# Counting a graph's edges band by band: the last turned tiles moved amid a band, the next band's bounds taken from this band's, and a first sum whose tiles follow their parts one by one

## The reference, cut to what matters

```python
out_deg = segment_sum(ones, src); in_deg = segment_sum(ones, dst)
h_src   = h * rsqrt(clip(out_deg, 1))[:, None]
agg     = segment_sum(h_src[src], dst)            # layer 0; the others sum likewise
agg     = agg * rsqrt(clip(in_deg, 1))[:, None]
out     = elu(agg @ weight + bias)
...
m   = segment_sum(xt[src], dst) * Binv[:, None]   # layer 2 sums there and back, twice
out = segment_sum(m[dst], src) * Dinv[:, None]
```

## Time and profile before

| what | value |
|---|---|
| median of 3 runs | 1943.09 us (1941.39 to 1947.62) |
| the profiled execution's own time | 1939.86 us |
| its span | 1938.1 us |
| TensorE, matmuls | 1755.6 us, 91% of the span |
| VectorE | 949.9 us, 49% |
| ScalarE | 482.1 us, 25% |
| GpSimd | 494.8 us, 26% |
| data moved | 535.59 MB, mean 276 GB/s |

### The profile page before, as it was taken

The page is one execution under the profiler, slowest core; times in us unless marked ns, Lnnn a source line. Parts: engine busy times, 40 slices in busy tenths (PEclk is TensorE's granted clock), DMA queues, the critical chain, the costliest instruction groups (busy, mean ns, idle before and its releaser), DMA issues.

```text
span 1938.1 us, 35033 instructions
## 1 busy us (share of the span) xinstructions
PE 1755.6 (91%) x9478; PEld 1416.2 (73%) x9479; DVE 949.9 (49%) x2851; ACT 482.1 (25%) x1262; POOL 494.8 (26%) x899
## 2 busy tenths in 40 slices
PE   4888887699989999999999999999999699999971
PEld 2355555588878878888887887887777589988851
DVE  7876664444446511122211117776777544444466
ACT  0134445322223211122221111112121133232223
POOL 1122222311113300000000002226888843332314
PEclk7999999799999999999999999999999799999986
DMA  5067778899969988887768889997777399999981
GB/s 135 34 280 310 321 332 356 302 323 324 307 225 374 346 292 290 264 226 214 211 196 289 289 269 278 290 287 245 266 251 264 124 307 371 371 372 371 374 308 67
DMA packets 339452, 535.59 MB, mean 276 GB/s; under 512 B 17871, under 2 KB 275322, under 8 KB 332442
## 3 DMA queue, kind: packets, MB, share of 16 engines
q1 hardware_dynamic: 329514, 516.24, 79.4%
q0 software_dynamic: 7888, 17.23, 2.4%
q10 hardware_dynamic: 1952, 0.95, 0.3%
HBM read 405.95 MB, written 128.41 MB: 276 GB/s over the span
## 4 chain that ended last, share of the span: by engine, by line
PE 63%; SPq 13%; DVE 7%; issue 7%; DMA 5%; DVEq 2%; POOL 1%; ACT 1%; ACTq 0%; POOLq 0%
PE psum L1118 44%; PE psum L1215 6%; SPq L486 4%; PE psum L1010 4%; PE psum L1007 3%; PE psum L1029 2%; SPq L500 2%; DMA blk<-counts_src_on_rows 2%; SPq L492 2%; SPq L496 2%; SPq L489 2%; PE psum L1197 2%; PE psum L1226 1%; SPq L827 1%; DMA expert_weights<-expert_rows_out 1%
## 5 line engine op out<-in xcount | busy, mean ns | idle before, releaser
L1118 PE MATMUL psum<-xsa,blk 128*128 128x512 f32 x2500 | 638.0, 403 | 12.3 <-DVE xsa L1684 9.1
L1118 PEld LDWEIGHTS psum<-xsa,blk 128*128 128x128 f32 x2500 | 456.6, 189 | 99.8 <-issue 12.0
L1118 PE MATMUL psum<-xsb,blk 128*128 128x512 f32 (+1 forms) x1875 | 407.8, 366 | 10.4 <-DMA blk<-counts_src_on_rows 5.8
L1118 PEld LDWEIGHTS psum<-xsb,blk 128*128 128x128 f32 x1875 | 315.7, 190 | 64.4 <-issue 10.2
L1966 POOL TENSOR_SCALAR ve<-mv 128x1 f32<-128x1 f32 x75 | 16.9, 225 | 763.0 <-DVE mv L1660 763.0
L1545 DVE TENSOR_SCALAR onehots<-counts_scratch 128x348 bf16<-128x348 f16 x464 | 162.3, 376 | 85.1 <-issue 44.8
L1007 PE MATMUL psum<-onehots 128*128 128x349 bf16 x464 | 147.7, 318 | 38.6 <-DVE onehots L1550 38.0
L1010 PE MATMUL psum<-zrow 128*128 128x512 bf16 x464 | 174.1, 385 | 0.0
L592 PE MATMUL psum<-route,expert_weights 128*128 128x128 f32 x1296 | 166.2, 282 | 2.6 <-DVE route L704 2.0
L592 PEld LDWEIGHTS psum<-route,expert_weights 128*128 128x128 f32 x1296 | 154.3, 195 | 12.3 <-issue 4.6
L604 PE MATMUL psum<-expert_weights,route 128*128 128x256 f32 x648 | 153.5, 380 | 0.2
(11 more groups left out here) (317 smaller groups left out, 2113.5 us busy)
## 6 DMA issues: line engine op xcount, KB each, us to landing
blk<-counts_src_on_rows SPq DMA_DIRECT2D x125, 832.0 KB, 5.8
blk<-counts_src_on_rows SPq DMA_DIRECT2D x125, 768.0 KB, 4.7
expert_weights<-in_L_gnn_w SPq DMA_DIRECT2D x162, 512.0 KB, 8.2
blk<-counts_dst_on_rows SPq DMA_DIRECT2D x50, 832.0 KB, 6.0
counts_dst_on_rows<-band_rows SPq DMA_DIRECT2D x25, 1600.0 KB, 5.9
blk<-counts_dst_on_rows SPq DMA_DIRECT2D x50, 768.0 KB, 5.6
counts_src_on_rows<-blk SPq DMA_DIRECT2D x13, 1600.0 KB, 6.7
counts_src_on_rows<-rblk SPq DMA_DIRECT2D x12, 1600.0 KB, 8.4
```

The costliest lines, as they stand in the source:

```text
L1118: mm = e.matmul(o, blk[n][:, k * P:(k + 1) * P], XS[:, k, :, 0:Fw], start=(k == 0), stop=(k == T - 1 and not own), skip_group_check=True)
```

## The change

It has three parts. TensorE's third round (7 tiles) stands amid the band together with the second (9 tiles), and nothing stands behind the second half. The next band's bounds come from a new function, `next_groups`, which takes the next band's `start` to be this band's `upto` and leaves out its extraction from the word; the function before is still used for band 0. In the first product of phase `l0` with i = 0 each matmul waits for its own part.

```diff
+        def next_groups(e, b, start):
+
+            v = e.value_load(tab[0:1, bass.ds(b, 1)], min_val=0, max_val=(1 << 30) - 1)
+            more = e.snap(e.to_reg((v >> 7) & 508), min_val=0, max_val=508)
+            middle = e.snap(e.to_reg((more & 504) + start), min_val=0, max_val=1 << 15)
+            upto = e.snap(e.to_reg(start + UNROLL + more), min_val=0, max_val=1 << 15)
+            return e.snap(e.to_reg((v & 511) - start), min_val=-(1 << 15), max_val=511), start, middle, upto
+
...
@@ -1040,14 +1048,14 @@
                 def amid():
                     middle()
                     if b + 1 < T:
-                        ends_of[1 - par] = groups_of(e, b + 1)
+                        ends_of[1 - par] = next_groups(e, b + 1, ends_of[par][3])
...
-            pipeline(e, [(2, turn_rounds(0, 1)), (2, turn_rounds(1, 2)), (2, turn_rounds(2, TURNS))], band, unrolled=True)
+            pipeline(e, [(2, turn_rounds(0, 1)), (2, turn_rounds(1, TURNS)), (2, nothing)], band, unrolled=True)
...
@@ -1101,7 +1109,9 @@
                     if before is not None and isinstance(i, int) and i == 0:
 
-                        if k in (0, lo):
+                        if ph == "l0":
+                            e.wait_ge(S("tile_part1"), past(before, "part1") + k + 1)
+                        elif k in (0, lo):
                             e.wait_ge(S("tile_part1"), past(before, "part1") + max(k + 1, min(hi, T - 8)))
...
```

## The result

The changed kernel takes 1915.87 us in the median of four runs (1914.28 to 1920.13), the one before 1942.84 us in the runs beside it: a ratio of 0.987, 95% interval 0.9847 to 0.9892. The forecast was 1918.4 us within 1912 to 1928.

What follows compares the result with a forecast made beforehand. Bound: counting, where TensorE and VectorE hand the chain to each other. 17.5 + 3.5 - 1.0 + 4.6 = 24.6 us off the profiled 1939.86 gives 1915.2; the median, 3.2 above, 1918.4 us; range 1912 to 1928.

Steps and rivals of the forecast that it cites:

- The seven moved tiles: At 22 band ends, seven turned tiles moved amid the band save 0.80 us each: 17.5 us (15 to 19).
- The cover amid the band: In a turn's middle the moved tiles fall into TensorE's 1.36 us wait for one-hots, of which 0.56 is left.
- The register steps: VectorE's bounds steps in the band's middle get 0.14 us shorter (0.09 to 0.23); 24 bands give 3.5 us (2.2 to 5.5).
- on the path since VectorE is the late one in the middle: In the band's middle TensorE waits for VectorE, so the 0.14 us saved in its register steps shortens every band.
- The stores and the tail: Turned bands' stores issue 1.7 us earlier, but backlog behind the counting costs up to 2.5 us: a loss of 1.0 us.
- The first product: In the sums' first product, matmuls follow their parts one by one, so read-out starts earlier: gain 4.6 us (2.0 to 4.8).
- the signs: Trace marks listed beforehand, among them the sums' first product starting 6 to 7 us before the last part.
- rival (2): In the sums' first product, gaps keep the clock at half until tile 2: gain 2.0 instead of 4.6, 1921; chance 0.08.
- Rival (1): Stores become the bound of the counting, with 371 GB/s perhaps the ceiling in the last light turns: 1921 to 1929; chance 0.11.
- Rival (3): Amid the band, ScalarE's copy waits for a late store and stalls TensorE and VectorE: slower, 1949; chance 0.03.
- Rival (4): VectorE's register steps save nothing, as the fused step of five may last 260 ns: 1920 to 1922; chance 0.05.
- The sign named for this rival: VectorE's "issue" idle amid the band staying at 1.75 us or more would show that the register steps save nothing.

## Why the prediction was right

Time, range and direction were right, and the sum of 24.6 us stands against 24.7 from the kernels with one part each and the tail (17.2 + 3.3 + 4.5, less 0.45, with 0.1 or 0.2 for turns 0 to 2). That the two agree to 0.1 is luck, since terms that were too high (0.3, 0.2 and 0.1) are offset by a loss put 0.55 too large, and the 27 us between the medians are not explained to the last 2. By its steps:

- **The seven moved tiles.** 0.78 us per band end for 0.80, 17.2 us for 17.5. The cover amid the band held, 0.49 us of wait left for 0.42. VectorE's wait at the start: 0.69 for 0.60.
- **The register steps.** The total was near (3.3 over turns 3 to 23 for 3.5), but by errors that offset each other. The sum of the steps was mis-sized: five fused operations took 160 ns, not 205, so that, with some 0.02 us less in the steps beside it, the steps are 0.23 us shorter and not 0.14, the edge of the range. And the step "on the path since VectorE is the late one in the middle" left out who else holds VectorE there. In a light turn only 0.10 arrived, as GpSimd's second cast ends where VectorE's one-hot would run. In the turns with 20 and 24 chunks nothing arrived, for the same reason. The turns with 16 chunks and two light ones gave 0.3 to 0.6; in part pauses of the sequencers went away there, which the prediction did not know of and whose cause is open.
- **The stores and the tail.** A loss of 0.45 us for 1.0. The 2.5 us that bounded this term do not follow from their own figures: the 414 GB/s worked out for the last light turns lie below 437, so that no backlog would be left. The 1.0 was a guess. The earlier issue and the longer landing were both there: the store of the earlier trace rows was issued 2.3 us after the last band's end and is now at 0.7, and takes 2.0 longer.
- **The first product.** 4.5 us for 4.6. The working gave 4.8, as it put 0.6 us between the last part's end and the read-out; it is 1.0 (344.23 to 345.24). The first matmul began 9.4 us before the last part's end, as 352.6 and 362.1 of the working say, and not the 6 to 7 us named among the signs. The clock rose within the first tile, at 338.0, and the second tile's read-out came 6.66 us behind the first's, before 6.62; rival (2) did not happen.
- **Rival (1).** The last turns moved 403 GB/s, above the 371 of the earlier trace rows, and from turn 7 on every turn with 12 chunks took 8.09 us (the last but one 8.20). 371 was demand, not a ceiling. The 358 GB/s of the Trainium skill (DMA: Bandwidth & Descriptors, section Where 436 GB/s comes from) did not bind here either, by the same 403.
- **Rival (3).** Its mechanism showed itself without its price: stores land 1.5 us later in the median (8.6 to 9.9 us after issue up to 296 us, where the limit worked out was 9.6), ScalarE waits for one 0.8 us at most, and TensorE waited for none of ScalarE's copies before the last band.
- **Rival (4)** was right in that something eats the gain of the steps, wrong in what: the fused step was cheaper than assumed, and "issue" idle fell to 1.52, below the 1.61 forecast. The sign named for this rival could not have shown the loss, as that sat in the length of the instruction behind.

## What to carry to other kernels

When an engine is made earlier, look not only at whom it waits for by semaphore but at the length of its next instruction: a stretched instruction is a wait that no view of waits lists. Look for it in the trace of before, in the places where the engine is early already: here five turns showed it. Where such a stretch ends at a constant distance behind another engine's instruction, try to shift work from that engine first, and then ask who receives it: here the gain came only after ScalarE's cast had been moved as well. An expected price multiplied by the number of turns is checked turn by turn, since three turns at a lower clock can hide in a sum that fits. With turns that repeat to 0.03 us, a single profile decides about 0.1 us per turn, where the totals of several runs can't tell 3 us.

## What was unexpected in the hardware

VectorE's one-hots and GpSimd's casts hold each other up, and whoever comes second ends at a constant distance behind the other. In all 13 profiles, that of before among them, a stretched source one-hot (0.372 us alone; 139 cases in turns 3 to 23) ended 0.102 to 0.108 us after a cast, whether it had begun 0.28 or 1.11 us before that end, and across casts of 0.48, 0.76 and 1.05 us. A destination one-hot (0.28 us alone, 16 cases) ended 0.139 to 0.143 us after one. A one-hot that began less than 0.27 us before the end of the cast was not stretched, which is the same finding: 0.372 less 0.105. The other way round, GpSimd's first cast runs beside VectorE's digits and takes 1.25 us, the second, of the same size, 1.05; the first ended 0.91 to 0.92 us behind the last digits in all turns from 3 on, and a whole second cast that began some 0.2 us behind a one-hot ended 0.91 us behind it and took 1.10.

This fits the shared pair of ports of the Trainium skill, SBUF — State Buffer, section Who interferes with whom: a lock for the whole instruction, on which the other fully blocks. The trace agrees that the second waits for the first. It does not show a whole instruction's length behind the release: the one-hot ends 0.10 us behind the cast and not 0.37, so its record begins before the point at which it is held, and where that point lies is not shown. In the run with the extra cast a one-hot whose record began up to 0.05 us ahead of the next cast's still came behind it, and one that began 0.23 us ahead came first.

The load of the bounds' word into VectorE's registers took 0.30 to 0.32 us in the turns without a store in flight, 0.88 to 0.93 us with two, and anything from 0.30 to 0.92 with one (909 ns on TensorE in the earlier trace rows); that the stores are the reason was not tested. The half clock came and went in turns 1 and 2 from one execution of the same kernel to the next.
